# A layer norm's inverse square root, moved from ScalarE's Ln and Exp to Newton steps on VectorE

## The reference

```python
def _layernorm(x, axis=-1, eps=1e-5):
    m = jnp.mean(x, axis=axis, keepdims=True)
    v = jnp.var(x, axis=axis, keepdims=True)
    return (x - m) / jnp.sqrt(v + eps)

# attn: per token, 16 heads of 64 attend to one another
qkv = (x @ W_qkv + b_qkv).reshape(B, S, 16, 192)          # D_MODEL = 1024
scores = einsum('bshd,bsgd->bshg', q, k) / sqrt(64)
context = einsum('bshg,bsgd->bshd', softmax(scores), v)
attn = context.reshape(B, S, 1024) @ W_out + b_out
# ffn: for each of 8 experts (hidden 4096), summed
acc += (silu(x @ wg) * (x @ wu)) @ wd

x = x + _layernorm(attn(_layernorm(x)))
x = x + _layernorm(ffn(_layernorm(x)))
```

## Time and profile before

| | us |
|---|---|
| median of 2 runs (7111.3 to 7111.39) | 7111.34 |
| the profiled execution's own time | 7139.37 |
| its span on the slowest core (core 3) | 7137.7 |
| spans of the 8 cores | 7105.0 to 7137.7 |
| PE busy | 5705.4 (80%) |
| DVE busy | 3204.4 (45%) |
| ACT busy | 779.9 (11%) |

### The profile page before, as it was taken

The page is one execution under the profiler, slowest core; times in us unless marked ns, Lnnn a source line. Parts: engine busy times, 40 slices in busy tenths (PEclk is TensorE's granted clock), DMA queues, the critical chain, the costliest instruction groups (busy, mean ns, idle before and its releaser), DMA issues.

```text
span 7137.7 us, 71349 instructions; the slowest of 8 cores (7105.0 to 7137.7 us)
## 1 busy us (share of the span) xinstructions
PE 5705.4 (80%) x26240; PEld 2566.0 (36%) x26240; DVE 3204.4 (45%) x4451; ACT 779.9 (11%) x1323; POOL 165.0 (2%) x202
## 2 busy tenths in 40 slices
PE   2112222218999999999999999999999999999992
PEld 0000000003444444444444444444444444444441
DVE  3666666663344343443433434434344343343436
ACT  0000000001111111111111111111111111111101
POOL 0000000000000000000000000000000000000000
PEclk8556666658999999999999999999999999999985
DMA  3000000004222232222232222223222223222212
GB/s 71 0 24 0 24 0 9 4 0 65 36 36 36 42 48 36 36 36 36 38 45 43 36 36 36 36 42 47 37 36 36 36 37 46 43 36 36 36 18 94
DMA packets 178221, 247.85 MB, mean 35 GB/s; under 512 B 3808, under 2 KB 134880, under 8 KB 177888
## 3 DMA queue, kind: packets, MB, share of 16 engines
q0 software_dynamic: 169056, 209.74, 20.2%
q1 hardware_dynamic: 8832, 33.56, 1.4%
HBM read 436.22 MB, written 16.78 MB: 63 GB/s over the span
## 4 chain that ended last, share of the span: by engine, by line
PE 80%; DVE 14%; issue 3%; ACT 2%; another core or an unknown queue 1%; DMA 0%; DVEq 0%; ACTq 0%; POOL 0%; POOLq 0%
PE ps_d L507 25%; PE ps_g L476 25%; PE ps_u L481 25%; PE ps_mm L235 3%; DVE prod L307 2%; DVE prod L265 2%; DVE prod L303 2%; DVE prod L261 2%; PE ps_att L337 1%; DVE stats L145 1%; ACT scr L143 1%; PE ps_tr L184 1%; DVE stats L141 1%; PE ps_mm L231 0%
## 5 line engine op out<-in xcount | busy, mean ns | idle before, releaser
L491 DVE TENSOR_TENSOR hbuf<-silb,ps_u 128x512 bf16<-128x512 bf16 x1024 | 704.3, 688 | 2904.9 <-PE ps_u L481 2866.4
L476 PE MATMUL ps_g<-ln2T,wg_b 128*128 128x512 bf16 x8192 | 1947.0, 381 | 33.8 <-DMA wd_b<-wd 33.8
L481 PE MATMUL ps_u<-ln2T,wu_b 128*128 128x512 bf16 x8192 | 1945.8, 381 | 0.0
L507 PE MATMUL ps_d<-hbuf,wd_b 128*128 128x512 bf16 x8192 | 1822.2, 381 | 0.0
L517 DVE TENSOR_TENSOR acc<-ps_d,acc 128x512 f32<-128x512 f32 x2016 | 1392.9, 691 | 343.4 <-PE ps_d L507 317.1
L476 PEld LDWEIGHTS ps_g<-ln2T,wg_b 128*128 128x128 bf16 x8192 | 803.9, 98 | 1009.0 <-issue 68.1
L507 PEld LDWEIGHTS ps_d<-hbuf,wd_b 128*128 128x128 bf16 x8192 | 804.5, 98 | 976.1 <-issue 41.1
L481 PEld LDWEIGHTS ps_u<-ln2T,wu_b 128*128 128x128 bf16 x8192 | 804.2, 98 | 974.4 <-issue 34.2
L487 ACT ACTIVATE silb<-ps_g 128x512 bf16<-128x512 f32 x1024 | 611.4, 597 | 4704.3 <-PE ps_g L476 4704.3
L184 PE MATMUL ps_tr<-ident,ctxt 128*128 128x128 bf16 x128 | 16.2, 306 | 917.2 <-DVE ctxt L315 917.2
L184 PEld LDWEIGHTS ps_tr<-ident,ctxt 128*128 128x128 bf16 x128 | 12.4, 137 | 921.2 <-issue 921.2
(11 more groups left out here) (71 smaller groups left out, 918.9 us busy)
## 6 DMA issues: line engine op xcount, KB each, us to landing
wg_b<-wg POOLq DMA_DIRECT2D x64, 1024.0 KB, 12.2
wu_b<-wu POOLq DMA_DIRECT2D x64, 1024.0 KB, 19.3
wd_b<-wd POOLq DMA_DIRECT2D x64, 1024.0 KB, 23.6
xf<-x SPq DMA_DIRECT2D x4, 2048.0 KB, 13.9
xspill<-xf SPq DMA_DIRECT2D x4, 2048.0 KB, 7.0
xrel<-xspill SPq DMA_DIRECT2D x16, 512.0 KB, 3.9
out<-outb SPq DMA_DIRECT2D x16, 512.0 KB, 2.9
wqkv_sb<-wqkv POOLq DMA_DIRECT2D x1, 6144.0 KB, 53.3
```

The costliest lines, as they stand in the source:

```text
L476: gt = op('t', lambda t, par=par, kh=kh, kd=kd, bk=bk, toks=toks: t.matmul(ps_g[:, bk], wg_b[:, par, kd, kh * 128:(kh + 1) * 128], ln2T[:, ...
L481: ut = op('t', lambda t, par=par, kh=kh, kd=kd, bk=bk, toks=toks: t.matmul(ps_u[:, bk], wu_b[:, par, kd, kh * 128:(kh + 1) * 128], ln2T[:, ...
L491: mul_tok[c] = op('v', lambda v, kh=kh, bk=bk, c=c, q=q: v.tensor_tensor(hbuf[:, q % 2, kh], silb[:, c % 2], ps_u[:, bk], ALU.mult), MUL)
L507: dt_ = op('t', lambda t, par=par, m=m, mi=mi, kh=kh, q=q: t.matmul(ps_d[:, mi], wd_b[:, par, kh, m * 128:(m + 1) * 128], hbuf[:, q % 2, k ...
```

## The change

`ln_stats` is split in two. The new `ln_stats`, for S1 and S7, squares its SBUF input with a product on DVE ahead of the sum, in place of ACT's Square. `ln_stats_psum`, for S6, keeps Square on ACT. In both, and in the last stage, Ln and Exp on ACT are replaced: DVE adds EPS, and `newton_rsqrt` makes a first guess from the bits of the variance (shift right by one, subtracted from a constant that is kept in a third column of `consts`) and refines it in three rounds of four instructions. Each of these instructions is followed by a wait for its own semaphore. Nothing else differs.

```diff
-    consts = S("consts", [128, 2], F32)
+    consts = S("consts", [128, 3], F32)
...
+    op('v', lambda v: v.memset(consts[:, 2:3], MAGIC), VV)
+
+    def newton_rsqrt(st_):
+        I32 = mybir.dt.int32
+        op('v', lambda v: v.tensor_scalar(st_[:, 3:4].bitcast(I32), st_[:, 2:3].bitcast(I32),
+                                          1, None, ALU.arith_shift_right), VV)
+        VV.wt('v')
+        op('v', lambda v: v.tensor_sub(st_[:, 4:5].bitcast(I32), consts[:, 2:3].bitcast(I32),
+                                       st_[:, 3:4].bitcast(I32)), VV)
+        VV.wt('v')
+        for _ in range(3):
+            op('v', lambda v: v.tensor_mul(st_[:, 6:7], st_[:, 4:5], st_[:, 4:5]), VV)
+            VV.wt('v')
+            op('v', lambda v: v.tensor_mul(st_[:, 6:7], st_[:, 6:7], st_[:, 2:3]), VV)
+            VV.wt('v')
+            op('v', lambda v: v.tensor_scalar(st_[:, 6:7], st_[:, 6:7], -0.5, 1.5,
+                                              ALU.mult, ALU.add), VV)
+            VV.wt('v')
+            op('v', lambda v: v.tensor_mul(st_[:, 4:5], st_[:, 4:5], st_[:, 6:7]), VV)
+            VV.wt('v')
 
     def ln_stats(src_fn, par):
+        st_ = stats[:, par]
+        op('v', lambda v: v.tensor_mul(scr[:, par], src_fn(), src_fn()))
+        op('v', lambda v: v.reduce_sum(st_[:, 0:1], src_fn(), axis=AX.X), VV)
+        VV.wt('v')
+        op('v', lambda v: v.reduce_sum(st_[:, 1:2], scr[:, par], axis=AX.X))
...
+    def ln_stats_psum(src_fn, par):
         st_ = stats[:, par]
         op('v', lambda v: v.reduce_sum(st_[:, 0:1], src_fn(), axis=AX.X), VV)
         VV.wt('s')
@@ -149,11 +189,10 @@
         op('v', lambda v: v.tensor_mul(st_[:, 2:3], st_[:, 0:1], st_[:, 0:1]), VV)
         VV.wt('v')
         op('v', lambda v: v.tensor_sub(st_[:, 2:3], st_[:, 1:2], st_[:, 2:3]), VV)
-        VV.wt('s')
-        op('s', lambda s: s.activation(st_[:, 3:4], st_[:, 2:3], AF.Ln, bias=consts[:, 0:1], scale=1.0), SS)
-        SS.wt('s')
-        op('s', lambda s: s.activation(st_[:, 4:5], st_[:, 3:4], AF.Exp, scale=consts[:, 1:2]), SS)
-        SS.wt('v')
+        VV.wt('v')
+        op('v', lambda v: v.tensor_scalar_add(st_[:, 2:3], st_[:, 2:3], EPS), VV)
+        VV.wt('v')
+        newton_rsqrt(st_)
         return op('v', lambda v: v.tensor_scalar(st_[:, 5:6], st_[:, 0:1], st_[:, 4:5], -1.0,
                                                  ALU.mult, ALU.mult), VV)
...
-        ln_stats(psa, p2)
+        ln_stats_psum(psa, p2)
```

More of the change, by code:

```diff
@@ L24 @@
 EPS = 1e-5
+MAGIC = float(np.int32(0x5F3759DF).view(np.float32))
 def build(mode='full', nt_lim=NT):
@@ L136, in build @@
     op('v', lambda v: v.memset(consts[:, 0:1], EPS))
-    op('v', lambda v: v.memset(consts[:, 1:2], -0.5), VV)
-    def ln_stats(src_fn, par):
+    op('v', lambda v: v.memset(consts[:, 1:2], -0.5))
+    op('v', lambda v: v.memset(consts[:, 2:3], MAGIC), VV)
[17 more added lines that the diff above has]
+            VV.wt('v')
+    def ln_stats(src_fn, par):
+        st_ = stats[:, par]
[3 more added lines that the diff above has]
+        op('v', lambda v: v.reduce_sum(st_[:, 1:2], scr[:, par], axis=AX.X))
+        op('v', lambda v: v.tensor_scalar_mul(st_[:, 0:1], st_[:, 0:1], 1.0 / D), VV)
+        VV.wt('v')
+        op('v', lambda v: v.tensor_scalar_mul(st_[:, 1:2], st_[:, 1:2], 1.0 / D))
+        op('v', lambda v: v.tensor_mul(st_[:, 2:3], st_[:, 0:1], st_[:, 0:1]), VV)
+        VV.wt('v')
+        op('v', lambda v: v.tensor_sub(st_[:, 2:3], st_[:, 1:2], st_[:, 2:3]), VV)
+        VV.wt('v')
+        op('v', lambda v: v.tensor_scalar_add(st_[:, 2:3], st_[:, 2:3], EPS), VV)
+        VV.wt('v')
+        newton_rsqrt(st_)
+        return op('v', lambda v: v.tensor_scalar(st_[:, 5:6], st_[:, 0:1], st_[:, 4:5], -1.0,
+                                                 ALU.mult, ALU.mult), VV)
+    def ln_stats_psum(src_fn, par):
         st_ = stats[:, par]
@@ L594, in build @@
         op('v', lambda v, st_=st_: v.tensor_sub(st_[:, 2:3], st_[:, 1:2], st_[:, 2:3]), VV)
[L595 to L599, removed]
+        VV.wt('v')
+        op('v', lambda v, st_=st_: v.tensor_scalar_add(st_[:, 2:3], st_[:, 2:3], EPS), VV)
+        VV.wt('v')
+        newton_rsqrt(st_)
         op('v', lambda v, st_=st_: v.tensor_scalar(st_[:, 5:6], st_[:, 0:1], st_[:, 4:5], -1.0,
```

## The result

| | before | after |
|---|---|---|
| fastest execution, us | 7108.7 | 7306.2 |
| profiled execution, us | 7139.4 | 7305.7 |
| spans of the 8 cores in it, us | 7105.0 to 7137.7 | 7300.5 to 7304.0 |
| ratio, with its 95% interval | | 1.0275 (1.0252 to 1.0297) |

The change makes the kernel 2.75% slower: about 7307 us where 7297 was forecast.

What follows compares the result with a forecast made beforehand. Engines taking turns bound the attention stage, a DVE chain the last; PE fills the FFN stage. 63 groups x 3.07 = 193.4, less 4.8 and 2.6, gave +186 us: 7297 us, range 7265 to 7340.

Steps and rivals of the forecast that it cites:

- The bound and the path: Attention and last stages: statistics groups lie on the path, so added microseconds lengthen the tile; FFN stage keeps its length.
- The replaced stretch: Ln and Exp on ACT with handoffs, L151 to L157: 1.04 us goes in all 64 groups.
- what the 16 steps cost: L151 to L157, each step waited: 11 x 0.26 + 5 x 0.25 = 4.11 us, a group 3.07 longer.
- Square to DVE: S1 and S7: product on DVE takes 2.46 us where 2.47 stood; worth 0.01 us, path does not grow.
- The exception at tile 0: S1(1) runs during the QKV matmuls, S4 starts earlier: gives back 4.8 us, its own 3.07 covered.
- Tables: Two table loads of 1.28 us, at tile 0 and in the last stage, leave the path: 2.6 us.
- waits cost nothing: Rival, L151 to L157: 16 steps at 0.07 make 1.12 us, not slower, 7109 us; chance 0.03.
- a part hides beside PE: Rival: S6's chain under its 13.78 us idle, 49 us would go, 7248 us, +1.9%; chance 0.02.
- Dear int32 steps: Rival in the statistics groups: all steps at 0.32, 4.08 us more a group, 7361 us; chance 0.02.
- alternating tables: Rival: S6's Square and S4's Exp each wait 1.28 us for a table load, 38 us, 7335 us; chance 0.04.
- a low clock over QKV: Rival, attention stage: QKV matmuls stay at PE's low clock, 10 us a tile, 150 in all, 7447 us; chance 0.01.
- Profile against median: Whole kernel: profile lies 28 us above the median 7111.3; difference carried over, profiled 7325 becomes 7297.

Runs made afterwards that it cites:

- the kernel with one round: Changed kernel with one Newton round in place of three: 7168.7 us against 7111.0 for the kernel before, ratio 1.008.
- that with waited products: Kernel before plus 15 unused 128x1 products, each waited for, ahead of L151 in each of 64 groups: undisturbed cores 7362.3 to 7369.0 us, +261.

## Where the prediction was right and where it failed, point by point

**The bound and the path: right.** FFN stage unchanged (-1.3 us), all of the loss in the two stages with statistics.

**The replaced stretch: right.** 1.04 us before in 47 of 48 groups of the attention stage, 1.05 on average.

**The step that failed: what the 16 steps cost.** The kind of cost was right, the term was too small. The sum had 4.11 us a group, from 0.25 and 0.26 read off starts rounded to 0.01 us. The trace of after has 0.259 from a TENSOR_SCALAR to the next step and 0.264 to 0.266 from most TENSOR_TENSORs, so that a group is 4.21, 2% more. On top of that come pauses of 0.2 to 0.35 us, which the sum put at nothing, such as this one, ahead of a product of the S7 that was shown:

```profile
716.10 0.16 DVE L146 TENSOR_TENSOR stats<-consts,stats 128x1 int32<-128x1 int32 x1
716.56 0.16 DVE L150 TENSOR_TENSOR stats<-stats 128x1 f32<-128x1 f32 x1 [0.30 <-DVE stats L146]
```

The mean over all 64 groups is 4.28 us, the commonest value 4.21. With 4.28 - 1.05 = 3.23 a group, 63 groups give 203.5 in place of 193.4, and less 7.4 the sum is 196, which is what core 4 shows. These two terms, 0.10 and 0.07 a group, are the 10 us between 7297 and 7307.

The pauses are not scattered by chance. They occurred before too (one group of 48 at 1.39), and in the trace of after they are at the same instructions on all 8 cores. Number the entries of DVE's queue in that trace, waits and other entries without busy time included, and set a mark at the first pause and at every 128th entry on either side of it: of the 1218 steps on DVE between two 128x1 instructions, 20 pass a mark, and all 20 hold a pause; none of the other 1198 does. Counted in the same way, it is 17 of 17 in the kernel with one round and 15 of 15 in that with waited products. A packet of 8192 bytes in the DMA queue q14, which the page of the profile calls "instruction", starts 1.0 to 1.6 us behind the start of the instruction before each pause. That fits a refill of DVE's instructions every 128 entries; no run changed the length of the queue alone, so this cause is argued and not shown.

**Square to DVE: right,** by the trace (2.46 against 2.47) and by the run that has it alone (-2 us).

**The exception at tile 0: right.** S1(1) ran under QKV as forecast. On core 4, S4 started 2.56 us earlier than before (95.85 against 98.41), though the evacuation ahead of QKV had come 1.87 later (78.70 against 76.83), which is S1(0)'s own growth less its table load, counted elsewhere in the sum. The two together are 4.4, where the sum had 4.8. On core 4 the stage starts at 67.7 us in both kernels, and the evacuation of tile 0's context transposes is 2.6 us earlier than before (ctxT at 147.8 against 150.4); the sum had 4.8 + 1.3 - 3.1 = 3.0.

**Tables: right.** Two loads in place of three, neither on a statistics group's path, none alternating.

**Rivals.** That waits cost nothing is refuted by 0.070 against 0.264 for the same instruction; the Trainium skill's statement (VectorE: DVE Perf Modes, "The DRAIN you can't avoid") that the semaphore after each instruction costs nothing extra does not hold for these 128x1 instructions. That a part hides beside PE did not happen in the kernel as changed, but is true of the place: with S1 moved there, nine microseconds of DVE work a tile left the path. Dear int32 steps, alternating tables and a low clock over QKV did not occur (the QKV matmuls were busy for 184.6 us, before for 184.9); the first eight wout matmuls ran low, the second eight in 1.90 to 2.1 us, so the 2.83 of the earlier trace rows did not come back.

**Profile against median.** I carried the difference of the profiled executions over to the median as it was. The 28 us by which the profile before lay above its other runs belonged to one die of that execution, two of its cores above all (7133.7 and 7137.7 us; core 4 had 7105.0), and the profile after has none of it: it took 7305.7, not 7325. Against the undisturbed cores the difference is 195 to 198 us. Carried as a ratio, the forecast would have been 7296, so nothing hung on that choice. The base of 7111.3 was the median of two executions, and the forecast speaks only of executions like these; it had nothing to say of the medians of 7499 and 8105 above.

## What to carry to other kernels

In this kernel a chain of tiny DVE instructions that each wait for the last one costs 0.26 us a link, almost four times what such instructions cost without waits (0.070); count links, not work, and compare with the one handoff to ACT and back that they replace (1.04 us for Ln and Exp). Here, moving such work to the idle engine paid only where that engine waited anyway, and the place for it is found by asking what stands in front of the awaited instruction in its queue: here S6's Square stood behind six evacuations, and changing the order, with S1's Square moved to DVE (worth 2 us by itself) and no Newton steps, gave 2.2%.

## What the runs showed of the hardware that I had not expected

DVE pauses for 0.2 to 0.35 us between two small waited instructions wherever one of the marks, 128 entries apart in its queue, falls between them; 18 of the 64 groups had one, 11 of them in the attention stage. Shift and subtraction on int32 views last the same 154 and 160 ns as f32 instructions of the same shape.
